# A perceiver layer on one core: tree paths by a tangent beside the gelu, features by three products, the layer norm as add and multiply, new orders, lags and PSUM banks

## The reference

```
x = x + xattn(layernorm(x), ctx)   # 16 heads of 64 over 128 context rows of 96
x = x + tree(layernorm(x))         # 16 heads, each with 5 path bits
x = x + experts(layernorm(x))      # 8 heads, 10 of 1024 experts each

def tree(x):
    paths = sigmoid(x @ Wp + bp)                        # per row, head and bit
    agree = pq * pk + (1 - pq) * (1 - pk)               # query row against key row
    sim   = cumprod(agree over the 5 bits).sum() / 5    # causal, then softmax
    return (softmax(sim) @ (x @ Wv)) @ Wo

def experts(x):
    # per head two lists of 32 key scores, top 10 of each, top 10 of their 100 sums
    h = gelu(x . w_down[best]) * softmax(best scores)
    return h @ w_up[best]

def layernorm(x): return (x - mean(x)) / sqrt(var(x) + 1e-5)
```

## Time and profile before

| what | us |
|---|---|
| median of 3 runs | 1072.67 (1072.32 to 1073.87) |
| span of the profiled execution, first to last instruction | 1070.5 |
| PE busy | 973.2 (91%) |
| PE weight loads busy | 763.0 (71%) |
| POOL busy | 893.0 (83%) |
| ACT busy | 874.9 (82%) |
| DVE busy | 872.4 (82%) |

### The profile page before, as it was taken

How to read it: one execution, slowest core, us unless ns; L and a number is a source line. 1 busy time by engine, 2 the same in 40 slices (tenths; PEclk the granted TensorE clock), 3 DMA queues, 4 the chain that set the end, 5 groups by cost and what they waited for, 6 DMA issues and landing times.

```text
span 1070.5 us, 35810 instructions
## 1 busy us (share of the span) xinstructions
PE 973.2 (91%) x12440; PEld 763.0 (71%) x12440; DVE 872.4 (82%) x2877; ACT 874.9 (82%) x2123; POOL 893.0 (83%) x935
## 2 busy tenths in 40 slices
...
DMA packets 70367, 27.25 MB, mean 25 GB/s; under 512 B 47312, under 2 KB 69936, under 8 KB 70192
## 3 DMA queue, kind: packets, MB, share of 16 engines
...
## 4 chain that ended last, share of the span: by engine, by line
DVE 38%; PE 29%; POOL 13%; issue 13%; ACT 6%; DVEq 1%; DMA 0%; POOLq 0%; ACTq 0%; SPq 0%
DVE mw L1002 10%; POOL wsum L1123 7%; PE psXT L398 7%; POOL p L1063 5%; PE psXT L420 5%; DVE cand L976 5%; DVE top L944 5%; PE psF L592 4%; DVE best L971 4%; DVE best L981 3%; ACT ew L790 3%; PE psXT L422 2%; DVE us L956 2%; DVE q L629 2%; DVE negmax L879 2%
## 5 line engine op out<-in xcount | busy, mean ns | idle before, releaser
L1123 POOL TENSOR_TENSOR wsum<-wsum,mw 128x1024 f32<-128x1024 f32 x192 | 452.8, 2359 | 3.1
L1002 DVE SCALAR_TENSOR_TENSOR mw<-psF,cut,ew 128x1024 f32<-128x1024 f32 x256 | 324.5, 1278 | 47.9 <-ACT ew L790 45.2
L790 ACT ACTIVATE ew<-psF,lnz 128x1024 f32<-128x1024 f32 x256 | 285.5, 1128 | 12.4 <-PE psF L592 9.3
L700 ACT ACTIVATE p<-psXT,negmax 128x128 f32<-128x128 f32 x512 | 184.0, 400 | 3.8 <-DVE negmax L879 3.7
L592 PE MATMUL psF<-sel,usT 128*128 128x512 f16 x512 | 158.5, 392 | 30.3 <-DVE mw L1002 27.7
L379 PE MATMUL psXT<-cT,q 96*128 96x128 f32 x1024 | 142.4, 282 | 14.3 <-ACT p L700 11.0
L379 PEld LDWEIGHTS psXT<-cT,q 96*128 96x128 f32 x1024 | 124.2, 191 | 43.6 <-ACT p L700 25.9
L1063 POOL TENSOR_TENSOR p<-p,rrow 128x512 f32<-128x512 f32 x128 | 130.3, 1037 | 25.9 <-DVE rrow L888 25.9
L700 ACT ACTIVATION_READ_ACCUMULATOR p<-psXT,negmax 128x1 f32 x512 | 123.9, 242 | 0.0
L420 PE MATMUL psXT<-pT,c 128*32 128x384 f32 x768 | 110.7, 501 | 2.0 <-ACT pT L625 2.0
L422 PE MATMUL psXT<-pT,c 128*32 128x128 f32 x768 | 108.5, 278 | 0.0
...
## 6 DMA issues: line engine op xcount, KB each, us to landing
...
```

The lines of the kernel that those rows point to most:

```text
L700: ins = act.activation(p[:, k, i, :], bank[BANK[f"x.s{k}"]][:, i * M:i * M + M], ACT.Exp, bias=negmax[:, k, i:i + 1], accum_out=rowsum[:, ...
L790: done(f"e.x{h}", act.activation(ew[:, h % NEW, :], bank[BANK[f"e.s{h}"]], ACT.Exp, bias=lnz[:, t % 4, h:h + 1]))
L1002: done(f"e.w{h}", dve.scalar_tensor_tensor(out=mw[:, h % NMW, :], in0=bank[BANK[f"e.s{h}"]], scalar=cut[:, t % 4, h:h + 1], in1=ew[:, h % ...
L1123: done(f"e.a{h}", pool.tensor_tensor(wsum[:, t % 2, :], mw[:, 0, :] if h == 1 else wsum[:, t % 2, :], mw[:, h % NMW, :], ALU.add))
```

## The change

- **Paths.** `t.path` moves from DVE to ACT: two tangents (`ACT.Tanh`, scale 0.5) straight from the logits, since tanh(z/2) = 2·sigmoid(z) − 1. `t.pexp`, the sum, the reciprocal and POOL's 2p − 1 are gone. The two table loads around the gelu become steps of their own, `a.open` and `a.close`, and between them stand `k.shift`, `x.w0`, `e.gelu`, `t.sb`, `x.w1`, `t.path` and `t.v`.
- **Features.** Three products on POOL in place of one scaling and five: the product of bits pairwise (32 numbers a row), their 16 combinations (256), and these times the last bit (256).
- **Layer norm.** DVE's last small instruction now subtracts two pairs and so leaves the negated mean and variance + 1e-5 in `nv`; POOL adds and multiplies where it subtracted and multiplied.
- **Orders and lags.** All five tables are new; the longest lag is 8 where it was 6. The one-time set-up of the key scores moves from `x.q1`/`x.w1` of tile 1 and `t.path` of tile 0 to `t.sim`, `t.exp` and `t.div` of tile 0.
- **Banks.** `BANK` now gives each step one of eight banks, or a pair (`TWO_BANKS`). `e.out` leaves the pairs for bank 3. The waits that free a bank are written anew.
- **Loads.** The four loads of a tile wait for the tile two before, and for their own last landing, instead of the use of the last tile.

```diff
+                act.activation(leaf[:, t % 2], z_ps[:, :, DEPTH - 1:DEPTH], ACT.Tanh, scale=0.5)
+                done("t.path", act.activation(path[:, t % 2, :, :, 1:3],
+                                              z_ps[:, :, 0:DEPTH - 1].rearrange("p h (g l) -> p h g l", g=2), ACT.Tanh,
+                                              scale=0.5))
...
             def gelu(t):
-                act.preload_act_table_set("gelu_and_others")
-                done("e.gelu", act.activation(gh[:, t % 2, :], bank[BANK["e.hid"]], ACT.Gelu))
-                act.preload_act_table_set("natural_log_exp_and_others")
+                done("e.gelu", act.activation(gh[:, t % 2, :], at("e.hid"), ACT.Gelu))
...
+            def gelu_table(t):
+                act.preload_act_table_set("gelu_and_others")
+            steps["a.open"] = gelu_table
+            def exp_table(t):
+                act.preload_act_table_set("natural_log_exp_and_others")
+            steps["a.close"] = exp_table
...
-                done(name, dve.tensor_scalar_add(mv[:, i, t % 2, 1:2], mv[:, i, t % 2, 1:2], 1e-5))
+                done(name, dve.tensor_tensor(nv[:, i, t % 2, :], mv[:, i, t % 2, 0:3:2], mv[:, i, t % 2, 1:4:2], ALU.subtract))
...
-                lp.link(dve.tensor_scalar_add(e_ps, e_ps, 1.0))
-                done("t.path", dve.reciprocal(path[:].rearrange("p h d -> p (h d)"), e_ps))
...
-                    done(name, pool.tensor_scalar(dst[:, t % 2, :], src[:, t % slots, :], mv[:, i, t % 2, 0:1],
-                                                  rstd[:, i, t % 2, 0:1], ALU.subtract, ALU.mult))
+                    done(name, pool.tensor_scalar(dst[:, t % 2, :], src[:, t % slots, :], nv[:, i, t % 2, 0:1],
+                                                  rstd[:, i, t % 2, 0:1], ALU.add, ALU.mult))
...
-                lf.link(pool.tensor_scalar(path[:], path[:], 2.0, -1.0, ALU.mult, ALU.add))
...
+                lf.link(pool.tensor_tensor(pt[:, :, :, 3:4], pt[:, :, :, 1:2], pt[:, :, :, 2:3], ALU.mult))
+                lf.link(pool.tensor_tensor(feat[:, :, 0:NF // 2].rearrange("p h (b a) -> p h b a", b=4),
+                                           pt[:, :, 1, :].unsqueeze(3).to_broadcast([128, AH, 4, 4]),
+                                           pt[:, :, 0:1, :].to_broadcast([128, AH, 4, 4]), ALU.mult))
+                done("t.feat", pool.tensor_tensor(feat[:, :, NF // 2:NF], feat[:, :, 0:NF // 2],
+                                                  leaf[:, t % 2].to_broadcast([128, AH, NF // 2]), ALU.mult))
...
-    "k.eb": 4, "t.pexp": 3, "t.v": 3, "k.lnz": 4, "e.x2": 4, "e.x1": 4, "x.e0": 2, "e.x0": 4, "x.e2": 2,
+    "e.x5": 5, "x.t1": 3, "x.t2": 3, "e.x3": 5, "k.high": 4, "y.u0": 3, "e.x4": 5, "y.u1": 3, "x.t3": 3,
```

More of the change, by code:

```diff
@@ L140, in build, with run @@
         depth = max(lag for order in (PE_ORDER, ACT_ORDER, DVE_ORDER, POOL_ORDER, SP_ORDER) for lag in order.values())
-        def run(steps, order, begun=(), once={}):
+        def run(steps, order, begun=(), once={}, longer={}):
             assert set(order) == set(steps), set(order) ^ set(steps)
@@ L150, in run @@
                         once[name, t]()
-                    if 0 <= t < NT and (name, t) not in begun:
+                    if 0 <= t < NT + longer.get(name, 0) and (name, t) not in begun:
                         steps[name](t)
@@ L521, in tree_out @@
                 pe.wait_ge(s["t.csb"], t + 1)
-                done("t.out", pe.matmul(bank[BANK["t.out"]][:, 0:D], actxT[:], awo[:], start=True, stop=True))
+                done("t.out", pe.matmul(at("t.out")[:, 0:D], actxT[:], awo[:], start=True, stop=True))
             steps["t.out"] = tree_out
             def xn3_turn(t):
-                pe.wait_ge(s["t.res"], t + 1)
+                after(pe, "x.t2", t + 1)
+                at_ends(pe, "t.path", t)
+                at_ends(pe, "t.v", t)
                 pe.wait_ge(s["k.norm"], t + 1)
-                done("k.turn", pe.transpose(bank[BANK["k.turn"]][:, 0:128], xn3[:, t % 2, :], ident[:]))
+                pe.wait_ge(s["k.norm"], t + 1)
+                done("k.turn", pe.transpose(at("k.turn")[:, 0:128], xn3[:, t % 2, :], ident[:]))
             steps["k.turn"] = xn3_turn
             def key_scores(t):
+                after(pe, "y.u0", t + 1)
+                at_ends(pe, "k.split", t - 1)
+                at_ends(pe, "k.shift", t - 1)
                 pe.wait_ge(s["k.high"], t + 1)
@@ L798, in _ @@
                                ACT.Copy, scale=QKSCALE).then_inc(own["setup_sb"], 1)
-            run(steps, ACT_ORDER, once={ACT_VO: setup_vo, ACT_KEYS: setup_keys})
+            ahead = abs(ACT_ORDER["e.gelu"] - ACT_ORDER["t.path"])
+            run(steps, ACT_ORDER, once={ACT_VO: setup_vo, ACT_KEYS: setup_keys}, longer={n: ahead for n in TABLES})
         @block.vector
```

306 lines of the change are left out of this document (141 added, 165 removed), and 23 rows, old and new, of tables (ACT_ORDER, BANK, DVE_ORDER, PE_ORDER).

## The result

The changed kernel takes 1035.14 us in the median of four executions (1032.55 to 1040.14), the kernel before 1073.27 beside it: a ratio of 0.965, with a 95% interval of 0.962 to 0.968. The forecast was 1015, the range 1001 to 1048. Sign and range hold; the forecast itself is 20 us too low. That the range holds is in part luck: the forecast alone allowed 1003 to 1034, and 1035.14 lies in the part of the range that was added for late sums on POOL, which did not come; the time is high for another reason, the start. The four executions, 1040.14, 1037.34, 1032.94 and 1032.55, have mean granted TensorE clocks of 0.964, 0.964, 0.972 and 0.973 of full speed; the profiled one is the first, so its time stands 5 over the median.

What follows compares the result with a forecast made beforehand. The prediction took a ring of waits of 31.13 us a round, through DVE, POOL's first sum and divisions, and PE, as the bound. Start and end 104.8 + 31 x 29.3 = 1013.1, plus 2.2: 1015 us, range 1001 to 1048.

Steps and rivals of the forecast that it cites:

- late sums on POOL: Rival: slow norms and products on POOL delay `k.inner` and `t.norm`; round 30.0 to 30.9, 1049 us; chance 0.13.
- The ring through DVE and ACT: `k.top` to `k.z` on DVE, `e.x2` to `e.x4` on ACT, `e.w4`, next `k.top`: 29.2 us a round.
- The table loads: On ACT around the gelu: `a.open` hidden in the wait for `k.split`, `k.eb` at 10.8 to 11.0 with 1.0 to spare.
- e0: In `x.e0`, a kernel step on ACT, not a run: said to queue behind `k.eb`, with `k.lnz` and all `e.x`.
- The norm: On POOL: add and multiply take 0.26 to 0.81 us, middle 0.53; `k.norm` adds 0.1 at 0.53, `t.norm` nothing.
- The divisions: On POOL, now ahead of `e.a1`: that sum's 2.35 us leave the way to `x.p1`.
- the old ring: Waits through DVE, POOL's `e.a1` and divisions, and PE back to `k.top`: one round of 31.13 us, said to be broken.
- Start and end: Lags mostly rotation, key set-up off the chain saves 2, `e.w7` ahead of `k.z` costs 1.2: together 104.8 us.
- the signs that were named: In the changed profile: `k.top` spacing 29.2 to 29.6, `k.shift` wait under 1.3, POOL near 27, first `k.top` near 62.
- The rival that the pipeline pays: Two more lags cost two more rounds at start and end: 1073 us; chance 0.06 together with PE as the bound.
- the loads cost their row: Against the rival that table loads hold ACT beyond their 1.28 us: round 30.9, 1065 us; chance 0.02.
- PE as the bound: Rival: PE keeps its 1.7 idle, round stays 31.1, 1071 us; chance 0.06 together with the pipeline paying.

Runs made afterwards that it cites:

- experiment 9: Changed kernel with the first table load, `a.open`, moved from ahead of `k.shift` to just ahead of `e.gelu`: median 1042.81 us, round 29.51.
- experiment 7: Changed kernel with the layer norm's second instruction back at subtract and multiply: median 1051.31 us, round 29.79.
- experiment 10: Changed kernel with `e.a1` on POOL moved back ahead of the three divisions: median 1134.07 us, round 32.47.
- experiment 11: Kernel before the change with only the three divisions moved ahead of `e.a1` on POOL: median 1161.59 us, round 33.87.
- experiment 1: Changed kernel with `x.stats` at lag 1 in place of 0 on DVE: median 1028.42 us, first `k.top` at 71.5.
- experiment 3: Changed kernel with the set-ups of key scores and down weights moved into engines' waits: median 1025.73 us, first `k.top` at 74.7.
- experiment 5: Changed kernel run again unchanged: median 1035.62 us, first `k.top` at 80.6.
- experiment 2: Changed kernel with a third slot for `x` and tile 2's load issued earlier, orders kept: median 1025.19 us, first `k.top` at 72.0.
- experiment 4: Changed kernel with `x.stats` a round later and the set-ups of key scores and down weights moved: median 1023.22 us.

## Why the prediction was right, and where it was wrong

**The ring through DVE and ACT: right in its steps, but tied with one through PE.** DVE and ACT in the changed kernel (timelines; start, us):

```profile
496.45 1.66 DVE L934 MAX8 top<-psXT 128x8 f32<-128x32 f32 x16
...
500.66 0.69 DVE L948 SCALAR_TENSOR_TENSOR us<-psXT,us 128x512 f16<-128x512 f32 x1
...
508.55 0.22 DVE L979 TENSOR_REDUCE z<-ebest 128x8 f32<-128x80 f32 x1
...
525.60 1.66 DVE L934 MAX8 top<-psXT 128x8 f32<-128x32 f32 x16
```

```profile
501.38 0.60 ACT L755 ACTIVATE cand<-psXT 128x512 f32<-128x512 f32 x1 [0.31 <-DVE us L948]
...
505.50 0.18 ACT L708 ACTIVATE leaf<-psXT 128x16 f32<-128x16 f32 x1 [0.42 <-PE psXT L457]
505.58 0.22 ACT L709 ACTIVATE path<-psXT 128x64 f32<-128x64 f32 x1
...
505.98 1.28 ACT L782 ACT_TABLE_LOAD   x1
507.28 0.27 ACT L762 ACTIVATE ebest<-best 128x80 f32<-128x80 f32 x1
...
509.33 2.12 ACT L790 ACTIVATE ew<-psF,lnz 128x1024 f32<-128x1024 f32 x2
...
523.15 1.14 ACT L790 ACTIVATE ew<-psF,lnz 128x1024 f32<-128x1024 f32 x1
```

From `k.top`'s start: `k.z` at 12.1 (forecast 12.0), `e.x2` at 12.9 (12.8), the end of `e.x4` at 27.8 (28.0), the next `k.top` at 29.15 (29.2). What the prediction did not have is that `y.res` waits for PE as well: `y.out` ends at 501.38, and DVE comes free at 501.35. The chain takes the way through PE, and the two are as long. Only the leg to `k.key` was added up on PE, not the one to `y.out`.

**The table loads: right.** ACT's wait ahead of `k.shift` went from 2.6 to 0.31; `k.eb` starts at 10.8 (estimate 10.8 to 11.0) and ends 1.0 before `k.z`, the 1.0 that was given. That was not the tightest place, though: `x.e0`, which stands behind `k.eb`, leaves ACT at 508.97, 0.07 before `k.lnz`, and experiment 9 shows the loss there. `k.eb` starts 0.02 after the load ends. The Trainium skill, ScalarE: Activation LUTs, What ACT_TABLE_LOAD costs, has a drain of about 1.38 with every switch; this trace does not agree.

**The two tangents** take 0.18 and 0.22, at the low end of 0.2 to 0.3. **The features** take 0.25 + 0.64 + 0.62 = 1.51 where 1.6 was held. **POOL** is busy for 26.2 of a round, forecast 26.6. Its small margin was right in size (0.2, measured 0.3) and in the wrong place: `k.inner` has 0.4 to spare (its last sum ends at 502.10, `k.cand` starts at 502.54), `k.cut` 0.3.

**The norm: one of two legs missed.** The instruction takes 0.45, inside 0.26 to 0.81. At 0.81 the prediction priced `k.norm` at 0.4 (measured 0.34) and `t.norm` at nothing, since `t.sb` waits for the gelu anyhow; experiment 7 shows 0.21 there.

**The divisions: needed, but not enough.** The sum left the way to `x.p1` and the old ring is gone, as forecast; experiment 10 shows that without this move the round is longer again, and experiment 11 that the move alone makes the kernel before slower.

**Start and end: the step that failed.** It said that the lags are mostly rotation, that tile 0 has the same list of steps, that the loads were not waited for, and that the key set-up leaves the chain: 2 less. The list of tile 0 is indeed the same. What an engine does *ahead* of these steps for later tiles is not: at lag 0, `x.stats` of tile 2 is issued ahead of `x.low` of tile 0, and in the first round loads are late. Of the signs that were named, the others came, but the first `k.top` near 62 did not. The 24.9 by which the start passed the forecast are, at their places (differences of single profiled executions, those of experiments 1 and 3 on another chip than that of experiment 5):

- 9.1 the wait for tile 2's load (80.6 to 71.5, experiments 5 and 1, both profiles at a mean clock of 0.973);
- 5.9 the set-ups on the chain (80.6 to 74.7, experiments 5 and 3), where the prediction expected the key scores to leave it; up to 1 of it is clock again, 0.89 against 1.00 from 60 to 90 us;
- 7.8 the low clock of the profiled execution (88.4 to 80.6);
- 2.1 left over: with both mended the start is about that of the kernel before (65.3 by the estimate, 65.5), without the saving of 2 that was forecast.

The end took 1.6 more than forecast; that was not followed up. The rival that the pipeline pays had the right place and the wrong mechanism: experiments 2 and 3 keep all lags, 1 and 4 all but that of `x.stats`, and the start goes back to 71.2 in experiment 4, at full clock to 65 or so by the estimate, that of the kernel before. The other rivals did not come: POOL's sums are out of the ring, no engine waits for `k.inner`, the loads cost their row, and PE as the bound would have kept 31.1.
